# Attention heads on Trainium2: seven bf16 products in 64-row halves of the array instead of nine (or eight) in column strips

## The chip, the cores and the metric

The kernel runs on one core of one Trainium2 chip. The metric is the device time of one execution in microseconds (us); three runs of the kernel before took 1992.37 to 1998.57 us, median 1994.11.

## The reference, cut to what matters

A chain of four layers on 2048 tokens of width 128. Layers 0 and 3 have multi-head attention with 16 heads of width 8 over all 2048 tokens (layer 0 without a mask, layer 3 causal with rotary positions); layers 1 and 2 have attention over wide heads and mixtures of experts. The change touches only the multi-head attentions:

```python
N_HEAD = 16
q = proj(Wq, bq)                 # (heads, 2048, 8)
k = proj(Wk, bk)
v = proj(Wv, bv)
scores = jnp.einsum('bhtd,bhsd->bhts', q, k) * scale
attn = jax.nn.softmax(scores, axis=-1)
out = jnp.einsum('bhts,bhsd->bhtd', attn, v)
```

## The kernel before

`attention_heads(layer, causal)` does one of these attentions. TensorE (PE) multiplies bf16 numbers, so every fp32 query and key is held as a sum of three bf16 parts, and a score is a sum over products of parts stacked in the contraction dimension: 3 x 3 parts x 8 = 72 rows (`STK`), and 3 more rows (75) that subtract the row maximum. For each head three things are made:

- **Maxima** (`fill`, tile `pM`): scores with queries as output rows, reduced over keys by VectorE (DVE) in `take`. Layer 0 uses only the first 64 of the 72 rows: one run is two blocks of 512 keys, block 0 from rows 0 to 63 of `ks`/`qs`, block 1 from rows 64 to 127 of the copies `kd`/`qd`, so that the two matmuls run in two halves of the array. There are 32 runs for each head and four banks (`FILLED`), that is room for two runs. Layer 3 has 40 runs of one block of 128 to 512 columns and three banks.
- **Scores** (`score_chunk`, tile `pS`, a ring of three banks): keys as output rows, 512 queries in a chunk. ScalarE (ACT) takes the exponential of each chunk into `probs`. A chunk may be scored when the exponential three chunks earlier is done. `by_columns` writes a chunk as four matmuls of 32 output columns each, all of them over rows 0 to 74. In layer 3 the maxima go through `by_columns` too, and a block on the diagonal gets a further product `ident_b` x `neg_below`.
- **Sums** (`sum_unit`, tile `pO`): the exponentials times the values in fp32, four chunks at once, each in its own strip of 32 columns over all 128 rows. It waits for the exponential of the fourth chunk of its unit.

A unit is four chunks and one sum: 16 units a head in layer 0, 10 in layer 3. The order of PE is written out in `one_head` of the tensor block: sum of unit u, then the four chunks that lie three ahead, with maxima of the next head (`ahead(u)`) at the places `behind`: in layer 0 both runs after the second score when u is even, after the first and after the third when u is odd. So the three chunks in the ring at the time of a sum are those of the next unit, and the fourth of that unit is the first score after the sum.

When the maxima of a head are complete they are split in three bf16 parts, turned by PE (`turn`), copied by ACT (`keep_rows`), and copied by SyncE (SP) into rows 72 to 74 of the query stack (`load_max_rows`, three DMAs, awaited as `rows_in` before the next head's first score). Nine chunks lie between the turn and that score. SP also loads the stacks of the head after next (`load_stacks`, 14 DMAs a head in layer 0, 8 in layer 3). For the first head of a layer `load_first_keys` issues key loads from SP and ACT; only the last of them waits for the memset of the rows of ones.

```python
TURN_AT = first_chunk[TURN_UNIT + 1] + RING     # 55 of 64 chunks in layer 0, 31 of 40 in layer 3
```

## Time and profile before

| what | value |
|---|---|
| median of 3 runs | 1994.11 us |
| span of the profiled execution | 1923.2 us |
| median less span: what lies around the span | 70.9 us |
| PE, DVE, ACT busy | 1697.7, 1435.9, 1143.8 us |
| one head of layer 0, steady | 40.21 us |
| one head of layer 3, mean of 14 | 26.23 us |

The busy time of PE is modelled: each matmul is shown with its way through the array, some 0.17 us beyond the time in which its columns enter. Distances between the starts of matmuls say more than their lengths. Changes are reckoned on the span and taken over to the median unchanged.

### The profile page before, as it was taken

The page shows a single profiled execution, that of the slowest core. Times are in us where ns is not written, and L with a number is a line of the kernel's source. Part 1 is how long each engine was busy: PE and PEld are TensorE (multiplying, and loading weights), DVE is VectorE, ACT ScalarE, POOL GpSimd, SP SyncE. Part 2 cuts the span into 40 slices and gives each one's busy share as a digit, 9 for nine tenths or more (in the row PEclk, how much of TensorE's full clock was granted, in tenths as well). Part 3 has the DMA queues.
Part 4 walks back from the last instruction along what each step waited for, and adds up shares of the span by engine and source line. Part 5 has one row for each costly group of instructions (what it writes and reads, how often), then busy time and mean ns, then how long its engine had stood idle before and what let it go on. Part 6 is the DMA issues. An engine that isn't in the chain of part 4 may idle for free. (4 is left out here: it accounts for less than half of the span.)

```text
span 1923.2 us, 44062 instructions
## 1 busy us (share of the span) xinstructions
PE 1697.7 (88%) x17529; PEld 802.7 (42%) x17529; DVE 1435.9 (75%) x2718; ACT 1143.8 (59%) x2262; POOL 307.7 (16%) x460
## 2 busy tenths in 40 slices
PE   3799999999999995889997798892779999999977
PEld 2222222222222222434444544781425555555556
DVE  5889999999999954665555507656779999999735
ACT  3268888888888894332222244452317777777754
POOL 0103000010000100000000345443012232210123
PEclk8789999999999998799997899996759999999988
DMA  4112111121111012033233269861511111111132
GB/s 143 36 30 81 63 55 51 55 81 64 55 51 34 28 28 59 33 66 106 95 89 144 69 225 333 268 186 48 191 33 30 33 37 37 34 36 36 28 76 70
DMA packets 78037, 154.52 MB, mean 80 GB/s; under 512 B 18684, under 2 KB 35964, under 8 KB 74136
## 3 DMA queue, kind: packets, MB, share of 16 engines
q1 hardware_dynamic: 63034, 121.38, 20.0%
q0 software_dynamic: 14384, 29.29, 4.9%
q8 instruction: 139, 2.28, 0.5%
q10 hardware_dynamic: 414, 1.04, 0.2%
q14 instruction: 66, 0.54, 0.1%
HBM read 102.23 MB, written 48.89 MB: 79 GB/s over the span
## 5 line engine op out<-in xcount | busy, mean ns | idle before, releaser
L856 ACT ACTIVATE heads_probs<-heads_pS 128x512 f32<-128x512 f32 (+3 forms) x1664 | 851.6, 573 | 187.9 <-PE heads_pS L725 172.2
L881 DVE TENSOR_REDUCE heads_run_max<-heads_pM 128x1 f32<-128x1024 f32 x512 | 592.6, 1216 | 54.6 <-PE heads_pM L747 53.3
L787 PE MATMUL heads_pO<-heads_probs,heads_vh 128*32 128x512 f32 (+2 forms) x3328 | 438.1, 570 | 3.2 <-ACT heads_probs L856 1.4
L725 PE MATMUL heads_pS<-heads_qs,heads_ks 75*32 75x512 bf16 (+3 forms) x4160 | 392.7, 370 | 3.8 <-ACT heads_probs L856 1.6
L892 DVE TENSOR_REDUCE heads_run_max<-heads_pM 128x1 f32<-128x512 f32 x384 | 246.7, 684 | 17.2 <-PE heads_pM L725 13.7
L725 PE MATMUL heads_pS<-heads_q_first,heads_ks 75*32 75x512 bf16 x2496 | 234.4, 377 | 7.9 <-ACT heads_probs L856 7.4
L725 PEld LDWEIGHTS heads_pS<-heads_qs,heads_ks 75*32 75x32 bf16 x4160 | 117.3, 95 | 171.2 <-issue 81.3
L725 PE MATMUL heads_pM<-heads_ks,heads_qs 72*32 72x512 bf16 (+3 forms) x1600 | 174.6, 359 | 1.1 <-DVE heads_run_max L892 0.5
L889 DVE CUSTOM_DVE_ANT_0 heads_masked_out<-heads_pM,heads_mask_end 128x128 bf16<-128x128 f32 (+3 forms) x256 | 120.7, 485 | 19.5 <-PE heads_pM L725 17.2
L787 PEld LDWEIGHTS heads_pO<-heads_probs,heads_vh 128*32 128x32 f32 x3328 | 106.7, 110 | 53.3 <-issue 7.1
L725 PEld LDWEIGHTS heads_pS<-heads_q_first,heads_ks 75*32 75x32 bf16 x2496 | 71.3, 95 | 122.4 <-ACT heads_probs L856 66.8
L1404 ACT ACTIVATE top_act_gate<-top_pG 128x512 f32<-128x512 f32 x68 | 40.6, 597 | 137.3 <-PE top_pU L1360 137.3
L617 POOL DMA_DIRECT2D k_head_out_dram<-heads_ot x120 | 62.9, 531 | 356.9 <-DVE heads_ot L912 230.4
L747 PE MATMUL heads_pM<-heads_ks,heads_qs 64*128 64x512 bf16 x320 | 114.3, 393 | 4.7 <-DVE heads_run_max L881 4.7
L747 PE MATMUL heads_pM<-heads_kd,heads_qd 64*128 64x512 bf16 x320 | 114.3, 393 | 0.0
L725 PE MATMUL heads_pM<-heads_ks,heads_q_first 72*32 72x512 bf16 (+3 forms) x960 | 106.7, 383 | 7.9 <-DMA heads_ks<-k_parts_dram 6.7
L1438 DVE TENSOR_TENSOR top_hidden<-top_act_gate,top_pU 128x512 f32<-128x512 f32 x68 | 46.7, 687 | 76.8 <-ACT top_act_gate L1404 76.8
L2115 POOL DMA_INDIRECT k_x_slots_dram<-k_xn,k_place_i x32 | 31.1, 973 | 381.6 <-DVE k_place_i L1984 358.3
L725 PE MATMUL heads_pS<-k_neg_below,k_ident_b 128*32 128x128 bf16 x1024 | 90.7, 222 | 0.0
L1616 DVE TENSOR_REDUCE second_row_max<-second_banks 128x1 f32<-128x2048 f32 (+15 forms) x16 | 20.7, 1291 | 90.4 <-PE second_banks L1574 90.4
L725 PEld LDWEIGHTS heads_pM<-heads_ks,heads_qs 72*32 72x32 bf16 x1600 | 62.5, 97 | 59.3 <-DVE heads_run_max L892 19.1
L747 PEld LDWEIGHTS heads_pM<-heads_ks,heads_qs 64*128 64x128 bf16 x320 | 29.6, 93 | 133.4 <-DVE heads_run_max L881 86.7
(388 smaller groups left out, 2369.0 us busy)
## 6 DMA issues: line engine op xcount, KB each, us to landing
top_weights<-k_comb_dram SPq DMA_DIRECT2D x128, 128.0 KB, 3.0
second_w<-in_L_W_dram SPq DMA_DIRECT2D x12, 1024.0 KB, 10.8
k_hid_slots_dram<-k_zeros SPq DMA_DIRECT2D x8, 1152.0 KB, 5.0
k_h_slots_dram<-second_work SPq DMA_DIRECT2D x48, 192.0 KB, 3.1
second_work<-k_hid_slots_dram SPq DMA_DIRECT2D x48, 192.0 KB, 4.3
k_parts_dram<-proj_part SPq DMA_DIRECT2D x12, 512.0 KB, 4.1
heads_ks<-k_parts_dram SPq DMA_DIRECT2D x63, 96.0 KB
heads_qs<-k_parts_dram SPq DMA_DIRECT2D x40, 96.0 KB
```

Source lines behind the costliest of these rows:

```text
L617: queue.dma_start(K.head_out[h, :, b * BLK:(b + 1) * BLK], ot[c][b * 32:b * 32 + HD + 1, 0, :])\
L725: mm = pe.matmul(out[cols, :], still[:, cols], moving, start=start, stop=stop)
L747: mm = pe.matmul(pM[:, bank_of(c, j, k), 0:w], (qs, qd)[k][c % ROUND][rows, i * P:(i + 1) * P], (ks, kd)[k][c % ROUND][rows, b * BLK:b * B ...
L787: mm = pe.matmul(pO[k * 32:k * 32 + VW, int(second), o:BLK], vh[c][:, t, :], probs[u % 2][:, k * BLK + o:(k + 1) * BLK], start=first_chunk ...
L856: act.activation(probs[u % 2][:, k * BLK + c0 - b * BLK:(k + 1) * BLK], pS[:, slot, 0:c1 - c0], ACT.Exp)\
L881: dve.reduce_max(run_max[:, i, blocks[0][0] // 2:blocks[0][0] // 2 + 1], both.rearrange("p k c -> p (k c)"), AX.X).then_inc(taken, 2)
L889: dve.tensor_tensor_reduce(masked_out[:, i % TPB, 0:w], pM[:, bank, 0:w], mask_end[:, BLK - w:BLK], 1.0, LOWEST, ALU.add, ALU.max, run_max ...
L892: dve.reduce_max(run_max[:, i, b:b + 1], pM[:, bank, 0:w], AX.X).then_inc(taken, 1)
L1404: act.activation(act_gate[:, m % 2, :], pG[:, m % 2, :], ACT.Silu).then_inc(gated, 1)
L1438: mix = dve.tensor_tensor(hidden[:, m % 2, :], act_gate[:, m % 2, :], pU[:, m % 2, :], ALU.mult)
L1616: chain(dve.reduce_max(self.row_max[:, i:i + 1], self.scores_row[:, 0:(i + 1) * P], AX.X))
L2115: pool.indirect_dma_start(out=K.x_slots[k], out_offset=bass.IndirectOffsetOnAxis(ap=K.place_i[:, c, t:t + 1], axis=0), in_=K.xn[:, t, :], ...
```

## The change

Seven products of parts take the place of nine: query parts 0, 1, 2 with key part 0, the same with key part 1, and query part 0 with key part 2, so 56 rows and 3 for the maximum. Each stack stands twice, in rows 0 to 63 and in rows 64 to 127 of the same tile, and `kd`/`qd` are gone. Every score and every maximum is one matmul of 59 or 56 rows and 128 columns, and successive ones go alternately to the two halves. The masked diagonal takes two products of 64 rows in the half of its score. In layer 0 both runs of maxima of a unit now always stand after the second score. Ten loads a head fill the stacks (half of the queries' rows in one DMA with a repeat), six DMAs bring the rows of the maximum, the rows of ones are set by two memsets, and every first key load waits for one of them.

```diff
-STK = PARTS * PARTS * HD
+PRODUCTS = (3, 3, 1)
+STK = sum(PRODUCTS) * HD
+HALF = 64
...
+            for to, at in ((slice(0, HALF), slice(HALF, P)), (slice(HALF, P), slice(0, HALF))):
+                dve.tensor_copy(K.ident_swapped[to, :], K.ident[at, :]).then_inc(made, 1)
+                dve.tensor_scalar(K.neg_below_swapped[to, :], masks[at, 1, :], NEG, None, ALU.mult).then_inc(made, 1)
...
+def query_loads(K, h):
+
+    yield 0, 2 * PARTS * HD, K.parts[0][h].rearrange("a d t -> (a d) t").unsqueeze(0).broadcast_to([2, PARTS * HD, T])
+    yield 2 * PARTS * HD, STK, K.parts[0][h, 0]
+
+
+def key_loads(K, h):
+
+    for part, n in enumerate(PRODUCTS):
+        at = sum(PRODUCTS[:part]) * HD
+        yield at, at + n * HD, K.parts[1][h, part].unsqueeze(0).broadcast_to([n, HD, T])
...
-        LOADS = 8 if causal else 14
+        LOADS = 10
...
+            half = (0, HALF)[turn]
+            queue.wait_ge(ones_set[0], turn + 1)
+            for row, end, src in key_loads(K, 0):
+                queue.dma_start(ks[0][half + row:half + end, :], src).then_inc(stacked[0], 16)
...
             def load_max_rows(c):
-                for a in range(PARTS):
-                    sp.dma_start(qs[c % ROUND][STK + a:STK + a + 1, :].rearrange("o (t c) -> o t c", c=P),
-                                 max_rows[a * NT:(a + 1) * NT, :]).then_inc(rows_in, 16)
+                for row in (STK, HALF + STK):
+                    for a in range(PARTS):
+                        sp.dma_start(qs[c % ROUND][row + a:row + a + 1, :].rearrange("o (t c) -> o t c", c=P),
+                                     max_rows[a * NT:(a + 1) * NT, :]).then_inc(rows_in, 16)
...
+            turns = itertools.cycle((0, HALF))
...
+                for k, (b, w) in enumerate(blocks):
+                    at = next(turns)
+                    rows = slice(at, at + STK)
+                    mm = pe.matmul(pM[:, bank_of(c, j, k), 0:w], qs[c % ROUND][rows, i * P:(i + 1) * P],
+                                   ks[c % ROUND][rows, b * BLK:b * BLK + w], start=True, stop=True)
...
-                mm = by_columns(pS[:, slot, 0:c1 - c0], ks[c % ROUND][0:STK + PARTS, u * P:(u + 1) * P],
-                                qs[c % ROUND][0:STK + PARTS, c0:c1], True, not diag)
+                at = next(turns)
+                rows, mask = slice(at, at + STK + PARTS), slice(at, at + HALF)
+                mm = pe.matmul(pS[:, slot, 0:c1 - c0], ks[c % ROUND][rows, u * P:(u + 1) * P],
+                               qs[c % ROUND][rows, c0:c1], start=True, stop=not diag)
                 if diag:
-                    mm = by_columns(pS[:, slot, 0:P], K.ident_b[:, :], K.neg_below[:, :], False, True)
+                    pe.matmul(pS[:, slot, 0:P], K.ident_b[mask, :], K.neg_below[mask, :], start=False, stop=False)
+                    mm = pe.matmul(pS[:, slot, 0:P], K.ident_swapped[mask, :], K.neg_below_swapped[mask, :], start=False,
+                                   stop=True)
...
-                        behind = [(len(new) // 2, 1 + 2 * i)[u % 2] for i in range(len(todo))]
+                        behind = [len(new) // 2] * len(todo)
...
-            dve.memset(ks[0][64:96, :], 1.0).then_inc(ones_set[0], 1)
+            for row in (HALF // 2, HALF + HALF // 2):
+                dve.memset(ks[0][row:row + HALF // 2, :], 1.0).then_inc(ones_set[0], 1)
```

PE in the middle of a layer-0 head, before: an even and an odd unit, from sum to sum (`32x512` is a strip of 32 output columns, `128x512` the whole width).

```order
L787 MATMUL heads_pO<-heads_probs,heads_vh 32x512 x4
L725 MATMUL heads_pS<-heads_qs,heads_ks 32x512 x4
L747 MATMUL heads_pM<-heads_ks,heads_qs 128x512
L747 MATMUL heads_pM<-heads_kd,heads_qd 128x512
L725 MATMUL heads_pS<-heads_qs,heads_ks 32x512 x8
L747 MATMUL heads_pM<-heads_ks,heads_qs 128x512
L747 MATMUL heads_pM<-heads_kd,heads_qd 128x512
L725 MATMUL heads_pS<-heads_qs,heads_ks 32x512 x4
L787 MATMUL heads_pO<-heads_probs,heads_vh 32x512 x4
```

The same place after the change: every unit reads so.

```order
L786 MATMUL heads_pO<-heads_probs,heads_vh 32x512 x4
L768 MATMUL heads_pS<-heads_qs,heads_ks 128x512 x2
L742 MATMUL heads_pM<-heads_ks,heads_qs 128x512 x4
L768 MATMUL heads_pS<-heads_qs,heads_ks 128x512 x2
L786 MATMUL heads_pO<-heads_probs,heads_vh 32x512 x4
```

The strips of the sum now stand alone between matmuls of half the rows; before, scores and sums were both in strips of 32 columns, and the maxima stood alone.

PE in layer 3, the last chunk of one unit with its mask, the sum, and the first chunks of the next, before.

```order
L725 MATMUL heads_pS<-heads_qs,heads_ks 32x384 x4
L725 MATMUL heads_pS<-k_neg_below,k_ident_b 32x128 x4
L725 MATMUL heads_pM<-heads_ks,heads_q_first 32x512 x4
L787 MATMUL heads_pO<-heads_probs,heads_vh 32x128 x2
L787 MATMUL heads_pO<-heads_probs,heads_vh 32x512 x2
L725 MATMUL heads_pS<-heads_qs,heads_ks 32x512 x4
L725 MATMUL heads_pM<-heads_ks,heads_q_first 32x256 x4
```

The same place after.

```order
L768 MATMUL heads_pS<-heads_qs,heads_ks 128x384
L771 MATMUL heads_pS<-k_neg_below,k_ident_b 128x128
L772 MATMUL heads_pS<-k_neg_below_swapped,k_ident_swapped 128x128
L742 MATMUL heads_pM<-heads_ks,heads_q_first 128x512
L786 MATMUL heads_pO<-heads_probs,heads_vh 32x128 x2
L786 MATMUL heads_pO<-heads_probs,heads_vh 32x512 x2
L768 MATMUL heads_pS<-heads_qs,heads_ks 128x512
L742 MATMUL heads_pM<-heads_ks,heads_q_first 128x256
```

Here everything was in strips before; now each sum again stands alone between matmuls of half the rows, and the order of the work is the old one.

## Rows read from the trace of the kernel before

**Rows 1.** Windows: a head of layer 0, the start of the last one, a head of layer 3.

```profile
core 0: us, PE busy (x) PEld busy (x) DVE busy (x) ACT busy (x) POOL busy (x), PEclk, DMA share, GB/s
340.90:381.11 40.21, 40.21 (x453) 11.53 (x452) 37.29 (x34) 35.37 (x67) 3.21 (x9) 1.00 0.18 61
700.00:716.00 16.00, 13.62 (x173) 4.15 (x169) 1.05 (x2) 14.98 (x31) 2.91 (x8) 1.00 0.06 14
1611.33:1637.39 26.06, 25.86 (x469) 14.41 (x468) 23.96 (x64) 19.02 (x42) 7.39 (x11) 1.00 0.13 35
```

**Rows 2.** Timeline, PE, two units of layer 0: start, length, what, count.

```profile
322.15 1.03 PE L787 MATMUL heads_pO<-heads_probs,heads_vh 128*32 128x512 f32 x8
323.01 0.39 PE L725 MATMUL heads_pS<-heads_qs,heads_ks 75*32 75x512 bf16 x4
323.33 0.39 PE L747 MATMUL heads_pM<-heads_ks,heads_q_first 64*128 64x512 bf16 x1
323.65 0.62 PE L725 MATMUL heads_pS<-heads_qs,heads_ks 75*32 75x512 bf16 x8
...
326.14 0.39 PE L747 MATMUL heads_pM<-heads_ks,heads_q_first 64*128 64x512 bf16 x1
...
326.37 0.38 PE L747 MATMUL heads_pM<-heads_ks,heads_q_first 64*128 64x512 bf16 x1
...
327.12 1.03 PE L787 MATMUL heads_pO<-heads_probs,heads_vh 128*32 128x512 f32 x8
```

**Rows 3.** Timeline, ACT and DVE, the same two units.

```profile
323.45 2.23 ACT L856 ACTIVATE heads_probs<-heads_pS 128x512 f32<-128x512 f32 x4 [0.21 <-PE heads_pS L725]
...
321.67 4.62 DVE L881 TENSOR_REDUCE heads_run_max<-heads_pM 128x1 f32<-128x1024 f32 x4 [0.36 <-PE heads_pM L747]
```

**Rows 4.** Timeline, last head of layer 0, where no maxima are left.

```profile
702.96 6.42 ACT L856 ACTIVATE heads_probs<-heads_pS 128x512 f32<-128x512 f32 x12
...
703.61 0.40 PE L725 MATMUL heads_pS<-heads_qs,heads_ks 75*32 75x512 bf16 x4 [0.27 <-ACT heads_probs L856]
...
703.83 1.03 PE L787 MATMUL heads_pO<-heads_probs,heads_vh 128*32 128x512 f32 x8
...
704.69 0.82 PE L725 MATMUL heads_pS<-heads_qs,heads_ks 75*32 75x512 bf16 x12
...
706.01 1.03 PE L787 MATMUL heads_pO<-heads_probs,heads_vh 128*32 128x512 f32 x8
```

**Rows 5.** Timeline, ACT's copies of the turned maxima: one a head.

```profile
139.85 0.27 ACT L837 ACTIVATE heads_max_rows<-heads_pS 48x128 bf16<-48x128 bf16 x1 [0.30 <-PE heads_pS L757]
...
662.57 0.27 ACT L837 ACTIVATE heads_max_rows<-heads_pS 48x128 bf16<-48x128 bf16 x1 [0.30 <-PE heads_pS L757]
...
1453.60 0.27 ACT L837 ACTIVATE heads_max_rows<-heads_pS 48x128 bf16<-48x128 bf16 x1 [0.71 <-PE heads_pS L757]
...
1820.81 0.27 ACT L837 ACTIVATE heads_max_rows<-heads_pS 48x128 bf16<-48x128 bf16 x1 [0.82 <-PE heads_pS L757]
```

**Rows 6.** Timeline, SP and PE, from the turned maxima to the next head's scores.

```profile
1611.62 1.82 SPq L639 DMA_DIRECT2D heads_qs<-heads_max_rows  x3
...
1611.07 0.22 PE L757 MATMUL heads_pS<-k_ident_b,heads_max_parts 128*128 128x128 bf16 x1
...
1616.06 0.60 PE L725 MATMUL heads_pS<-heads_qs,heads_ks 75*32 75x512 bf16 x4
```

**Rows 7.** The tile of the maximum's rows, whole run: time to landing.

```profile
DMA to landing us min/median/max: 1.6/1.7/4.7
```

**Rows 8.** Timeline, starts of layer 0's and of layer 3's heads.

```profile
47.34 2.07 ACTq L600 DMA_DIRECT2D heads_kd<-k_parts_dram  x3
...
47.83 1.76 DVE L917 MEMSET heads_ks<- 32x2048 bf16 x1 [3.47 <-PEq L65]
49.46 0.60 ACT L974 ACTIVATE heads_probs<-heads_pS 128x512 f32<-128x512 f32 x1 [11.00 <-PE heads_pS L958]
...
1401.71 1.85 PE L725 MATMUL heads_pM<-heads_ks,heads_q_first 72*32 72x128 bf16 x24 [6.71 <-DMA heads_ks<-k_parts_dram]
```

More of the change, by code:

```diff
@@ L7 @@
+import itertools
 from contextlib import ExitStack
@@ L462, in _ @@
                     dve.tensor_tensor(dst, src, bv.unsqueeze(1).broadcast_to([P, TPB, D]), ALU.add).then_inc(vkept, 1)
-HALF = 64
-PRODUCTS = ((0, 0, 3), (1, 0, 3), (2, 0, 2), (2, 2, 3))
-def first_queries(K, causal):
-    at = 0
-    for _, n0, n1 in PRODUCTS:
-        rows = at + (n1 - n0) * HD
-        for first in (0,) if causal or at >= HALF else (0, HALF):
-            yield K.first_q[first // HALF][first + at:first + rows, :], K.parts[0][0, n0:n1].rearrange("a d t -> d a t")
-        at = rows
+def query_loads(K, h):
[5 more added lines that the diff above has]
+        yield at, at + n * HD, K.parts[1][h, part].unsqueeze(0).broadcast_to([n, HD, T])
+def first_queries(K, causal):
+    for half in (0, HALF):
+        for row, end, src in query_loads(K, 0):
+            yield K.first_q[half + row:half + end, :], src
 def causal_plan(causal):
@@ L581, in load_stacks @@
         def load_stacks(p, c):
[L583 to L600 removed]
+            h = ROUND * p + c
+            for half in (0, HALF):
+                for row, end, src in query_loads(K, h):
+                    yield qs[c % ROUND][half + row:half + end, :], src, stacked[c % ROUND]
+                for row, end, src in key_loads(K, h):
+                    yield ks[c % ROUND][half + row:half + end, :], src, stacked[c % ROUND]
+        def load_first_keys(queue, turn):
+            half = (0, HALF)[turn]
+            queue.wait_ge(ones_set[0], turn + 1)
+            for row, end, src in key_loads(K, 0):
+                queue.dma_start(ks[0][half + row:half + end, :], src).then_inc(stacked[0], 16)
         def split_max(queue, g):
@@ L661, in _ @@
             load_max_rows(0)
-            sp.wait_ge(ones_set[2], 1)
+            sp.wait_ge(ones_set[2], 2)
             every_head(one_head)
@@ L705, in _ @@
             for i in range(1, ROUND):
-                pool.memset(ks[i][64:96, :], 1.0).then_inc(ones_set[i], 1)
-                pool.wait_ge(ones_set[i], 1)
+                for n, row in enumerate((HALF // 2, HALF + HALF // 2)):
+                    pool.memset(ks[i][row:row + HALF // 2, :], 1.0).then_inc(ones_set[i], 1)
+                    pool.wait_ge(ones_set[i], n + 1)
             for i in range(ROUND):
@@ L720, in _ @@
         def _(pe):
-            def by_columns(out, still, moving, start, stop):
-                for g in range(P // VW):
-                    cols = slice(g * VW, (g + 1) * VW)
-                    mm = pe.matmul(out[cols, :], still[:, cols], moving, start=start, stop=stop)
-                return mm
+            turns = itertools.cycle((0, HALF))
             def bank_of(c, j, k):
```

45 lines of the change are left out of this document (9 added, 36 removed).

## The prediction

> **What bounds the kernel now.** I read the windows of one head in each of the two layers first, then the timeline of PE within it, then ACT and DVE beside it. In layer 0 a head takes 40.21 us and PE is shown busy for all of it, DVE for 37.29, ACT for 35.37 [rows 1]. Since the busy time of PE is modelled, I count distances between starts. A chunk of scores takes 0.22 (703.61 to the sum at 703.83), a sum 0.86 (703.83 to 704.69) [rows 4], a pair of maxima 0.23 (326.14 to 326.37) [rows 2]. From scores to maxima it is 0.32 (323.01 to 323.33) and from maxima to scores again 0.32 (323.33 to 323.65) [rows 2], so PE loses some 0.10 wherever strips of 32 columns and halves of rows meet, and nothing between scores and sums, which are both strips. Two units then hold 8 x 0.22 + 2 x 0.86 + 4 x 0.22 + 6 x 0.10 = 4.96 us; from sum to sum over two units the trace shows 327.12 - 322.15 = 4.97 [rows 2]. PE is the limit and waits for nobody. DVE takes four runs in 4.62 and stands idle 0.36 [rows 3], 2.31 a unit; PE's unit is 2.485.
>
> In layer 3 a head takes 26.06 with DVE busy for 23.96 and ACT for 19.02 [rows 1]; the mean of 14 heads is (1820.81 - 1453.60) / 14 = 26.23 [rows 5]. All of PE's work there is in strips, without any change of form, and DVE has only 2.1 us of air. Layer 0's steady heads are 13 intervals of (662.57 - 139.85) / 13 = 40.21 [rows 5].
>
> **Layer 0, work of PE.** Two successive scores, or a pair of maxima, now run in two halves, and the maxima show the price: 0.22 for two [rows 2]. A unit is 0.86 for the sum, 4 x 0.22 for eight halves and two changes of form around the sum, 1.94 us in place of 2.485. That is below DVE's 2.31 and below ACT, whose twelve exponentials take 6.42, so 0.54 apiece and 2.16 a unit [rows 4]. Whether the change gives 2.31 is decided by a chain, not by a sum of work.
>
> **Layer 0, the chain through the sum.** Call T the end of the last exponential of a unit. The score that takes its bank and the sum behind it both wait for T. The last head, which has no maxima, shows this chain in strips: exponential from 702.96, 0.60 long as the exponential in [rows 8] is, to 703.56; score 703.61; sum 703.83; next score 704.69 [rows 4]; ACT starts 0.44 after a score (323.01 to 323.45) [rows 2, 3] and ends 0.60 later. So 0.05 + 0.22 + 0.86 + 0.44 + 0.60 = 2.17, and from sum to sum it is 706.01 - 703.83 = 2.18 [rows 4]. After the change the sum is a strip form between two half forms, so 0.10 is lost ahead of it and 0.10 behind it, both on this chain: 2.38 us. This exceeds DVE's 2.31, and I take it as the new unit. The maxima fit: both runs stand behind the second score after the sum, some 1.5 us after T, and DVE needs the first of them about 2.0 after T; the second can wait for its banks until 2.1, since the last score of the unit waits for the next T anyway. A head is 16 x 2.38 plus the 0.45 that the turn costs now (40.21 - 16 x 2.485), 38.5: 1.7 less, for 15 heads -25.6. The last head has no maxima to gain by and goes from 2.18 to 2.38 a unit: +3.2. Layer 0: -22.4.
>
> The price of the change of form around an fp32 sum is not in the trace; the nearest rows are strips to halves and back in bf16, 0.10 each [rows 2]. Its bounds are 0, if weights and columns of the next form can enter while the sum runs out, and the whole way through the array, 0.39 - 0.22 = 0.17 [rows 2]. I take 0.10. The Trainium skill (TensorEngine Tiling (Array Packing), Key Properties) says that changing the tiling mode drains TensorE. By that rule each sum pays twice; the trace agrees for the maxima, with 0.10 a change. The same skill's page TensorE: Matmul & The Clock Gate (LDWEIGHTS) makes a weight load as long as its columns, an estimate of 107 ns for 128 and 27 ns for 32 columns; no sum here needs it.
>
> **Layer 3.** Per unit up to four maxima stand behind the scores, one of them just ahead of the sum. The chain was 0.05 + 0.44 (score and maximum) + 0.86 + 0.44 + 0.60 = 2.39; after, score and maximum run together (0.22) and two changes come in (0.20): 2.37, the same. What is gained is work of PE, so that maxima stand ready earlier; DVE's 23.96 a head [rows 1] bounds that, at about 24.3 with the turn. Against it: on a diagonal block the second mask product has to follow the first in the same half, where four strips worked at once, so the blocks with masks (16 a head) no longer pair with the maximum behind them; and DVE's three banks are not refilled during a sum, now 1.06 long. Between 24.3 and 27.0 I take 25.7, -0.5 for 15 heads, -7.5. The last head: ten units at +0.20, +2. Layer 3: -5.5.
>
> **The rows of the maximum.** Three DMAs take SP 1.82 to issue [rows 6], 0.61 each; three more put the last issue at 1611.62 + 5 x 0.61 = 1614.67, and it lands 1.7 later [rows 7], at 1616.4, where the next head's first score stood at 1616.06, 4.99 after the turn at 1611.07 [rows 6]. In layer 0 the chain puts that score about 5.0 after the turn, too. The wait of 0.3 to 0.4 lies ahead of two scores that wait for a later exponential anyway, with some 0.5 of air, so a median landing costs nothing; the longest was 4.7 [rows 7] and there are now twice as many. I put +2 for the whole kernel; the bound is 0.4 for 30 heads, +12. Queued behind them on SP are only loads that are needed a head later.
>
> **The starts.** First key loads wait for memsets of 1.76 each [rows 8], the second one done 3.5 after DVE starts; ACT, which issued its loads from 47.34 and did its first exponential at 49.46 [rows 8], now starts issuing about 51.4 and is free at 53.4, 4 us later. Part of this hides behind PE's slow first products, so I take +2.6 in layer 0, where 0 and 4 are the ends. Four query loads in place of seven let the stage before end some 1 earlier: -1. In layer 3 PE waited for the keys until 1401.71 [rows 8] with nothing beside it: one more memset and one more issue by ACT, +3.4 (1.76 + 0.61 at the least). Four small operations of DVE on the constants: +0.5. Fewer rows are loaded a head in layer 0 and more in layer 3, all a head ahead: nothing. Starts: +5.5.
>
> **The sum.** -22.4 - 5.5 + 2 + 5.5 = -20.4 us on the span of 1923.2, so 1902.8; with the 70.9 around it, the median of 1994.11 becomes 1974 (-1.0%). About 0.3%, 6 us, is what a measurement of this kernel can tell from no change.
>
> **The rivals.**
>
> *DVE's floor is reached* (15 in 100). If halves can enter while the sum runs out, the chain is 2.18 and DVE's 2.31 counts: heads of 37.6 in layer 0 (-2.6 x 15 = -39), no loss in the last ones, and 24.5 in layer 3 (-1.7 x 15 = -26); with +7.5 this gives 1937. For it: two pairs of one form follow each other at 0.23 [rows 2]. Against it: every change of form that the trace shows cost 0.10.
>
> *Layer 3 gives back what layer 0 gains* (17 in 100). If DVE starves during the sums and masks block the maxima, a head takes 27.0: +0.8 x 15 + 2 = +14, and 1994.11 - 22.4 + 14 + 7.5 = 1993, no change. For it: DVE has 2.1 us of air in a head of ten units [rows 1], and a sum with its two changes, during which nothing reaches it, grows by 0.20 a unit, 2.0 in all. Against it: before, a maximum waited behind each score, and now it runs beside it.
>
> *Slower: the change of form around the sums is dearer* (22 in 100). There are 16 x 16 + 16 x 10 = 416 sums with two changes each, 832 in all, nearly all on the chain. At 0.15 instead of 0.10 that is +42: 2015. It decides from 0.125 on, where the gain of 20.4 is gone. For it: fp32 needs two passes of weights for a sum, each shown as four loads, which the bf16 changes don't have. Against it: the weight loads of both kinds are short beside the columns.
>
> *The clock of PE falls.* It was 1.00 of 2.4 GHz with PE entering columns for (0.86 + 0.88) / 2.18 = 80% of the time in the last head [rows 1, 4]; after, it is 1.74 / 2.38 = 73%. I give this 1 in 100: at 1.2 GHz a unit of layer 0 would be about 3.6 us.
>
> **How the numbers follow.** The forecast has 45 in 100, DVE's floor 15, no gain 17, slower 23 with the clock in it. The forecast's own range is 1962 to 1986, by 0.09 to 0.115 a change of form. The whole range, leaving 8 in 100 of the floor and 11 of the slower case outside, is 1948 to 2008. Faster by over 0.3%: 0.45 + 0.15 + some 0.02 of the third case = 0.62; within 0.3%: the other 0.15; slower: 0.23.
>
> **What would show it.** In a middle head of layer 0: sums 2.38 apart, 0.32 from a score's start to the sum and 0.96 from the sum to the next score, intervals of 38.5 between copies of the turned maxima, DVE busy 37.3, PE's start distance of successive scores near 0.01 where both banks are free. In layer 3: intervals near 25.7, more waits of DVE for maxima during sums. At the heads' starts 2.6 and 3.4 later first maxima, counted from the stage's start. The prediction is wrong if sums in layer 0 are 2.31 or over 2.45 apart, or if layer 3's heads grow.

## The result, and the profile after

The changed kernel takes 2004.12 us (median of 5 runs, 1996.05 to 2005.03), the kernel before 1994.11 on the same chip: ratio 1.0051 [1.0032, 1.0071]. It is slower by 10 us where the prediction said 1974.0, 20 faster. On another chip, where the kernel before takes 1924.12, it takes 1950.55: 1.0139 [1.0116, 1.0161]. The chips of all experiments below take 1924 to 1926 us for the kernel before, and the span of 1923.2 in the rows ahead of the prediction fits such a chip and not the one of the result. The "70.9 us around the span" were therefore no part of the program but the distance between two chips: the profiled execution of the changed kernel has a span of 1994.2 in 1996.05, and the kernel before has one of 1922.1 in 1923.95 (e4), so 1.9 lie around it. Times below are set against the kernel before on the same chip.

Windows of a head of layer 0 and of one of layer 3, changed kernel (columns as in [rows 1]):

```profile
350.00:389.30 39.30, 35.94 (x261) 7.78 (x257) 37.51 (x34) 33.90 (x67) 3.21 (x9) 1.00 0.16 57
1706.68:1732.63 25.95, 23.31 (x195) 7.66 (x194) 23.92 (x64) 18.51 (x41) 3.45 (x7) 1.00 0.13 42
```

PE's work is smaller (35.94 in 39.30, where it filled 40.21 [rows 1]), and the head is 0.9 shorter, not 1.7. Timeline of PE, one unit in the middle of a head of layer 0, against [rows 2]:

```profile
320.71 1.07 PE L786 MATMUL heads_pO<-heads_probs,heads_vh 128*32 128x512 f32 x8
321.71 0.39 PE L768 MATMUL heads_pS<-heads_qs,heads_ks 59*128 59x512 bf16 x2
321.93 0.91 PE L742 MATMUL heads_pM<-heads_ks,heads_q_first 56*128 56x512 bf16 x4
322.67 0.49 PE L768 MATMUL heads_pS<-heads_qs,heads_ks 59*128 59x512 bf16 x2
323.10 1.07 PE L786 MATMUL heads_pO<-heads_probs,heads_vh 128*32 128x512 f32 x8
```

From sum to sum it is 2.39, from a sum to the next score 1.00 in place of 0.86. ACT and DVE beside it, against [rows 3]: ACT waits 0.33 once a unit, and DVE runs on without a gap that the view shows.

```profile
322.13 2.06 ACT L855 ACTIVATE heads_probs<-heads_pS 128x512 f32<-128x512 f32 x4 [0.33 <-PE heads_pS L768]
```

```profile
320.04 11.92 DVE L880 TENSOR_REDUCE heads_run_max<-heads_pM 128x1 f32<-128x1024 f32 x10
```

The last head of layer 0, against [rows 4]: 2.39 from sum to sum where it was 2.18, with nothing but scores and sums on PE. A score is followed by the sum 0.32 later (717.08 to 717.40) and the sum by a score 0.99 later.

```profile
714.69 0.39 PE L768 MATMUL heads_pS<-heads_q_first,heads_ks 59*128 59x512 bf16 x1 [0.47 <-ACT heads_probs L855]
715.01 1.06 PE L786 MATMUL heads_pO<-heads_probs,heads_vh 128*32 128x512 f32 x8
...
717.08 0.39 PE L768 MATMUL heads_pS<-heads_q_first,heads_ks 59*128 59x512 bf16 x1 [0.47 <-ACT heads_probs L855]
717.40 1.06 PE L786 MATMUL heads_pO<-heads_probs,heads_vh 128*32 128x512 f32 x8
718.39 0.60 PE L768 MATMUL heads_pS<-heads_q_first,heads_ks 59*128 59x512 bf16 x3
```

The rows of the maximum, SP and PE, against [rows 6]: six issues take 4.17, and the first score of the next head that needs them waits 0.92.

```profile
190.66 4.17 SPq L643 DMA_DIRECT2D heads_qs<-heads_max_rows  x6
...
196.38 0.39 PE L768 MATMUL heads_pS<-heads_qs,heads_ks 59*128 59x512 bf16 x1 [0.92 <-DMA heads_qs<-heads_max_rows]
```

The start of layer 0's heads, against [rows 8]: two memsets instead of one and from 52.30 on (47.83 before), ACT's loads at 56.34 and its first exponential at 58.35 (49.46 before), and PE's first maxima at 66.63, after a wait of 4.79 for the keys.

```profile
52.30 1.76 DVE L917 MEMSET heads_ks<- 32x2048 bf16 x1 [6.88 <-PEq L68]
54.55 1.76 DVE L917 MEMSET heads_ks<- 32x2048 bf16 x1 [0.48 <-issue]
...
56.34 1.97 ACTq L603 DMA_DIRECT2D heads_ks<-k_parts_dram  x3
58.35 1.57 ACT L974 ACTIVATE heads_probs<-heads_pS 128x512 f32<-128x512 f32 x3 [18.84 <-issue]
...
66.63 1.04 PE L742 MATMUL heads_pM<-heads_ks,heads_q_first 56*128 56x512 bf16 x4 [4.79 <-DMA heads_ks<-k_parts_dram]
```

ACT's copies of the turned maxima, one a head, are milestones; the first of layer 0 and the last of layer 3 (against [rows 5]):

```profile
107.75 0.27 ACT L836 ACTIVATE heads_max_rows<-heads_pS 48x128 bf16<-48x128 bf16 x1 [19.26 <-PE heads_pS L752]
...
1888.44 0.27 ACT L836 ACTIVATE heads_max_rows<-heads_pS 48x128 bf16<-48x128 bf16 x1 [0.73 <-PE heads_pS L752]
```

Read in this way, the span of each kernel falls into five stretches. This table, in us, is worked out from those rows and the spans, one execution of each kernel, all on chips where the kernel before takes 1924 to 1926:

| kernel | to first | 15 heads, layer 0 | last of 0 to first of 3 | 15 heads, layer 3 | rest | span |
|---|---|---|---|---|---|---|
| before (e4) | 94.8 | 607.0 | 722.3 | 396.9 | 101.1 | 1922.1 |
| changed (e5) | 107.5 | 594.8 | 738.3 | 405.3 | 102.4 | 1948.3 |
| old form of loads (e1) | 99.0 | 595.9 | 730.6 | 399.4 | 102.3 | 1927.3 |
| starts relieved (e6) | 95.3 | 593.4 | 727.7 | 402.1 | 103.3 | 1921.8 |
| rows by half (e7) | 95.6 | 585.6 | 727.9 | 396.1 | 103.5 | 1908.7 |
| e7, old layer 3 (e8) | 95.8 | 586.0 | 725.9 | 398.7 | 101.0 | 1907.3 |
| full strips at the sums, apart (e15) | 96.2 | 575.6 | 723.8 | 398.0 | 103.1 | 1896.8 |

Three kernels whose layer 3 runs unchanged code (e4, e8, and the profile ahead of the prediction) differ by up to 2.5 us in its heads (396.2 to 398.7), so a difference of that size between two rows says nothing. The heads of layer 0 do get shorter (-12.2), the way to the first of them 12.7 longer, that to layer 3's first 16.0, and layer 3's heads 8.4 longer. The theory with which I went into the experiments: the mechanism in layer 0 is the predicted one, and what eats it is how the stacks and the rows of the maximum are brought. The rival: the matmuls in halves are themselves dearer than thought.

### The profile page after: what moved, and what is told of

Same layout as the page of the kernel before. It is cut to its first block and busy times, and to the rows that moved or that the text cites. A ratio compares the mean times of both kernels' runs of the same rounds, so it can differ in the third digit from the quotient of the medians.

```text
span 1994.2 us, 29288 instructions
## 1 busy us (share of the span) xinstructions
PE 1618.9 (81%) x10105; PEld 647.7 (32%) x10105; DVE 1446.2 (73%) x2724; ACT 1117.0 (56%) x2262; POOL 314.4 (16%) x464
## 5 line engine op out<-in xcount | busy, mean ns | idle before, releaser
L768 PE MATMUL heads_pS<-heads_qs,heads_ks 59*128 59x512 bf16 (+3 forms) x1040 | 263.5, 373 | 28.8 <-ACT heads_probs L855 13.3
L742 PE MATMUL heads_pM<-heads_ks,heads_qs 56*128 56x512 bf16 (+3 forms) x1040 | 248.2, 380 | 40.4 <-DVE heads_run_max L880 13.6
L742 PE MATMUL heads_pM<-heads_ks,heads_q_first 56*128 56x512 bf16 x624 | 157.1, 399 | 57.4 <-DMA heads_ks<-k_parts_dram 27.1
L768 PE MATMUL heads_pS<-heads_q_first,heads_ks 59*128 59x512 bf16 x624 | 160.7, 379 | 21.2 <-ACT heads_probs L855 17.4
L768 PEld LDWEIGHTS heads_pS<-heads_qs,heads_ks 59*128 59x128 bf16 x1040 | 75.9, 93 | 289.8 <-ACT heads_probs L855 264.4
L742 PEld LDWEIGHTS heads_pM<-heads_ks,heads_qs 56*128 56x128 bf16 x1040 | 64.1, 94 | 138.7 <-DVE heads_run_max L880 105.0
L768 PEld LDWEIGHTS heads_pS<-heads_q_first,heads_ks 59*128 59x128 bf16 x624 | 45.1, 94 | 185.7 <-ACT heads_probs L855 173.3
L786 PEld LDWEIGHTS heads_pO<-heads_probs,heads_vh 128*32 128x32 f32 x3328 | 66.1, 108 | 98.2 <-issue 79.1
L1359 PE MATMUL top_pG<-k_xnT,k_gate 128*128 128x512 f32 x128 | 67.0, 606 | 4.2 <-PEq L68 4.2
L1368 PE MATMUL top_pY<-top_hidden,k_down 128*128 128x512 f32 x128 | 65.8, 595 | 1.6 <-DVE top_hidden L1444 1.6
```

What stands on the lines that cost most here:

```text
L742: mm = pe.matmul(pM[:, bank_of(c, j, k), 0:w], qs[c % ROUND][rows, i * P:(i + 1) * P], ks[c % ROUND][rows, b * BLK:b * BLK + w], start=Tru ...
L768: mm = pe.matmul(pS[:, slot, 0:c1 - c0], ks[c % ROUND][rows, u * P:(u + 1) * P], qs[c % ROUND][rows, c0:c1], start=True, stop=not diag)
L786: mm = pe.matmul(pO[k * 32:k * 32 + VW, int(second), o:BLK], vh[c][:, t, :], probs[u % 2][:, k * BLK + o:(k + 1) * BLK], start=first_chunk ...
L1359: pe.matmul(pG[:, m % 2, :], gw, x, start=True, stop=True)
L1368: pe.matmul(pY[:, b % 2, :], w, hidden[:, m % 2, :], start=(n == 0), stop=(n == L1_J)).then_inc(downed, 1)
```

## The experiments

All are compared with the kernel before on their own chip.

**e1, the loads alone put back.** The stacks keep the new halves, but their rows are ordered as before, so that each load has 8 as its outermost dimension (12 loads a head).

```diff
-    yield 0, 2 * PARTS * HD, K.parts[0][h].rearrange("a d t -> (a d) t").unsqueeze(0).broadcast_to([2, PARTS * HD, T])
-    yield 2 * PARTS * HD, STK, K.parts[0][h, 0]
+    for part, n in enumerate(PRODUCTS):
+        at = sum(PRODUCTS[:part]) * HD
+        yield at, at + n * HD, K.parts[0][h, 0:n].rearrange("a d t -> d a t")
...
-        yield at, at + n * HD, K.parts[1][h, part].unsqueeze(0).broadcast_to([n, HD, T])
+        yield at, at + n * HD, K.parts[1][h, part].unsqueeze(1).broadcast_to([HD, n, T])
```

> The changed kernel with its stack loads in the form of the kernel before: each load takes its rows with the eight head dimensions outermost (12 DMAs a head in place of 10), so that it isn't two or three long rows of packets. Theory 'loads': in the changed kernel's trace the first keys of layer 0 were awaited until 66.6 us (55.3 before) while 26 packets of 159 ns landed in each 2 us, about two of 16 DMA engines at work; the stores of the key parts ended the stage before 4.5 us later; in layer 3 the rows of the maximum were awaited up to 3.3 us. All this is the form of the loads: this run should be 15 to 30 us below the changed kernel, that is 1975 to 1990, with layer 0's first turned maxima near 100 us instead of 107.75. Rival 'memsets and more DMAs for the rows of the maximum': the loads' form is innocent, the waits stay, 2000 to 2006.

Measured 1933.3 us, ratio 1.0041 [1.0024, 1.0058], where the changed kernel has 1.0139: the form of the loads costs 18.5 us (medians less those of their own kernel before) or 21 (spans). At layer 0's start PE gets its first maxima at 58.85 after a wait of 0.74 for the keys; in e5 it was 67.03, after 3.27. Windows of 54 to 60 us show why (columns as in [rows 1]; the seventh is the share of the 16 DMA engines), first the changed kernel, e5:

```profile
54.00:60.00 6.00, 3.09 (x5) 1.03 (x4) 1.56 (x3) 1.57 (x3) 5.71 (x10) 0.78 0.22 67
```

and then e1:

```profile
54.00:60.00 6.00, 3.99 (x12) 1.50 (x12) 0.64 (x1) 3.37 (x6) 2.90 (x8) 1.00 0.45 158
```

67 GB/s against 158 with loads of the same stacks under way: 0.22 of 16 is 3.5 engines busy for the queues of SP and ACT together, 0.45 is 7.2. The window does not meet the same point of both starts, since SP issues its first key load at 53.18 in e5 and at 50.18 in e1; but later it is no better in e5:

```profile
60.00:64.00 4.00, 3.75 (x5) 1.01 (x3) 0.00 (x0) 1.40 (x3) 0.08 (x1) 0.50 0.24 83
```

Of the 8.2 us by which PE gets its maxima later, 3.0 lie ahead of the stage: its first memset starts at 51.39 in e5 and at 48.39 in e1. In the stage before, the first query loads and the stores of the key parts are under way together, and the slowest store lands 9.6 us after its issue in e5 (tile `k_parts_dram`, 28 to 52 us),

```profile
DMA to landing us min/median/max: 3.8/4.4/9.6
```

and 6.9 in e1:

```profile
DMA to landing us min/median/max: 3.8/4.3/6.9
```

**e2, the places of the maxima alone**, in the kernel before: `behind = [len(new) // 2] * len(todo)`.

> The kernel before with one part of the change alone: in layer 0 both runs of maxima always stand behind the second score. By the count of form changes (0.10 us each, two fewer per unit of odd number: 4 instead of 6 for two units) a unit falls from 2.485 to 2.385 us, a head of layer 0 from 40.2 to 38.6, in all -1.6 x 15 = -24 us: 1970. If form changes weren't what the time goes to, or DVE starves with both runs in one place, no change or slower: 1994 or more.

Measured 1936.0, ratio 1.005 [1.0031, 1.0068]: slower, and my expectation fell. Timeline of PE, e2:

```profile
362.69 0.39 PE L747 MATMUL heads_pM<-heads_ks,heads_qs 64*128 64x512 bf16 x1
362.69 0.39 PE L747 MATMUL heads_pM<-heads_kd,heads_qd 64*128 64x512 bf16 x1
363.18 0.39 PE L747 MATMUL heads_pM<-heads_ks,heads_qs 64*128 64x512 bf16 x1
```

The second run follows 0.49 after the first, not 0.23. Its weight load shows what it waits for, a bank that DVE is still reducing:

```profile
363.17 0.09 PEld L747 LDWEIGHTS heads_pM<-heads_ks,heads_qs 64*128 64x128 bf16 x1 [0.39 <-DVE heads_run_max L881]
```

PE, which was the limit, waits with it, in every second unit (in the others the second run follows after 0.26). Heads take 40.87.

**e3, the places alone put back**, in the changed kernel.

> The changed kernel with the maxima of layer 0 at the old places (after the second score, or after the first and the third). In 64-row halves a maximum costs no change of form, so the place should not matter to TensorE, and by the chain through the sum (2.38 us a unit) the time stays that of the changed kernel within 3 us (2001 to 2007). If the placement carries the gain of layer 0 by giving VectorE its banks together, this one is over 5 us slower.

Measured 1951.96, ratio 1.0132 [1.0114, 1.015], where the changed kernel has 1.0139: the places are worth nothing there, since a unit in the old places takes 2.39 too. That is what a chain through the sum asks for, and not a limit by DVE or by PE's work.

**e4 and e5, both kernels again.**

> The kernel before, unchanged, for its profile beside the others. The profile shown of it has a span of 1923.2 us where its timed runs took 1992 to 1999, and the changed kernel's profile has 1994.2 for a time of 1996.05. If the shown profile was an execution of another kind, this one shows where the 70 us lie (between the layers' heads: 783 us from the last turned maxima of layer 0 to the first of layer 3 in the changed kernel, 722 in the profile shown of before); if it is again near 1923, the 70 us lie around the span.

Measured 1923.95, with a span of 1922.1. The span is again near 1923, but the time is as well, so the 70 us lie between the chips and not around the span.

> The changed kernel once more, unaltered, beside the kernel before and the three below on one chip, as their base. Its parts so far: layer 0's heads -9 to -11 us, last head of layer 0 and start of layer 3 +17, start of layer 0 +8 to +12. Expected 9 to 14 us over the kernel before of the same chip, with the first turned maxima of layer 0 some 12 us later than before and of layer 3 some 17 us later counted from the last of layer 0. If it stands within 3 us of the kernel with the old form of loads (+8), the form of the loads costs nothing and that theory falls.

Measured 1950.55, 26 us over the kernel before, beyond what I expected. Against e1 the first turned maxima are 8.5 later, the way to layer 3 is 7.7 and its heads are 5.9 longer.

**e6, the starts relieved** (on e1): half of the ones is set by POOL beside DVE, key part 0 waits for no ones, and in layer 0 SP issues all first keys.

> The loads in the old form (six of the queries and six of the keys a head, outermost dimension 8), and the starts relieved: the ones of the second half are set by POOL beside DVE, only the loads of key parts 1 and 2 wait for ones, and in layer 0 all first keys are issued by SP, so that ACT is free. Theory that the two memsets and ACT's late issues are on the path: layer 0's first turned maxima 3 to 4 us earlier than with the loads alone (which stood 4.3 behind the kernel before), layer 3's 2 to 3 earlier; in all 4 to 6 less than the loads alone, about +2 to +4 against the kernel before. Rival, that the path at the starts goes through the stage before and the arrival of the keys: no more than 1 us.

Measured 1925.68, ratio 1.0009 [0.9999, 1.0019]: 6.3 us less than e1 by the medians less those of their own kernel before, 5.5 by the spans, 3.8 of it at layer 0's start. The start of layer 0 now stands 0.5 behind the kernel before.

**e7, rows by half** (on e6): two semaphores, one for each copy of the maximum's rows; a score waits for that of its own half, and the half that is needed first is issued first.

```diff
-                if n == 0:
-                    pe.wait_ge(rows_in, 32 * PARTS * (h + 1))
+                if n <= 1:
+                    half = HALF_OF[h, n]
+                    pe.wait_ge(rows_in[half // HALF], 16 * PARTS * (h + 1))
```

> As the kernel with relieved starts, and a score waits only for the three rows of the maximum of its own half; the half of the head's first score is brought first. Theory that six loads of rows in a row (some 4.1 us on SP) make PE wait once a head: the waits for rows go from about 1.0 to 0.2 us a head in layer 0, the interval of heads from 39.4 to about 38.8 to 39.0; in all 6 to 10 us less than the kernel with relieved starts, so 3 to 7 under the kernel before. Rival, that ACT's four copies of the sums and the turn set the end of a head: the interval stays at 39.3 or above and the time within 2 us.

Measured 1911.69, ratio 0.9938 [0.9916, 0.9959]: 14 us less than e6 and faster than the kernel before. Waits of PE's weight loads for the rows between 110 and 720 us (us in total, times, longest), e6:

```profile
PEld heads_pS L773 <- DMA heads_qs<-heads_max_rows: 10.0, 10, 1.7
```

and e7:

```profile
PEld heads_pS L809 <- DMA heads_qs<-heads_max_rows: 2.7, 5, 0.9
```

Every third head has its queries in `heads_q_first`, where the waits go from 3.4 in 5 to 1.3 in 3.

The heads of layer 0 settle at 38.64, a hair over the 38.5 of the prediction; layer 3's 15 heads take 6.0 less.

**e8, layer 3 as before the change** (on e7: nine products in strips there, three rows of the maximum).

> Layer 0 as in the kernel with rows by half; layer 3 wholly as before the change (72 and 75 rows in strips, single stacks, three rows of the maximum, 8 loads, no swapped constants). Theory that layer 3 gains nothing from the change and loses at its start and in its early heads: layer 3's first turned maxima again as far from layer 0's last as before plus 2 to 3 for layer 0's last head (722 to 725 us), intervals 26.0 as before; in all 8 to 13 us less than the kernel with rows by half, and 10 to 18 under the kernel before. If it is less than 4 under the kernel with rows by half, layer 3 in the new form costs nothing and the loss lies elsewhere.

Measured 1909.45, ratio 0.9925 [0.9905, 0.9944]; only 2.2 less than e7, and my expectation of 8 to 13 fell. Once loads and rows are mended, layer 3's heads take 396.1 in the new form (e7) and 398.7 in the old one, where the old one took 396.9 in e4, so no gain can be told from the scatter; around them the new form takes some 4.5 more.

**e9, strips around the sums** (layer 0, on e7): the score ahead of a sum and the one behind it are four strips of 32 columns over 59 rows.

```diff
+                if strips:
+                    mm = by_columns(pS[:, slot, 0:c1 - c0], ks[c % ROUND][rows, u * P:(u + 1) * P],
+                                    qs[c % ROUND][rows, c0:c1], True, not diag)
...
-                            score_chunk(p, d, n)
+                            score_chunk(p, d, n, strips=not causal and k in (0, len(new) - 1))
```

> On the kernel with rows by half: in layer 0 the score just ahead of each sum and the one just behind it are written as four strips of 32 columns over their 59 rows, the other two scores of the unit and the maxima stay whole in halves. So the two changes of form of a unit no longer touch the sum. Theory that the two changes around the sum lie on the chain at 0.10 each: the last head's unit falls from 2.39 to 2.18, in the other heads the chain falls to 2.18 too and DVE (about 2.31 a unit) or PE decides, so heads of 37.3 to 37.7 in place of 38.64; in all 16 to 22 us less than the kernel with rows by half. Rival, that something else (bank waits for DVE, ACT) holds the unit at 2.39: the last head falls, the others do not, 3 us less.

Measured 1972.54, ratio 1.0239 [1.0219, 1.0259]: 59 us more than e7 by medians, 62 by spans, the opposite of what both theories said. Timeline of PE, e9:

```profile
323.33 0.38 PE L823 MATMUL heads_pS<-heads_qs,heads_ks 59*128 59x512 bf16 x1
323.64 0.40 PE L771 MATMUL heads_pS<-heads_qs,heads_ks 59*32 59x512 bf16 x4
323.96 1.07 PE L841 MATMUL heads_pO<-heads_probs,heads_vh 128*32 128x512 f32 x8
324.96 0.40 PE L771 MATMUL heads_pS<-heads_qs,heads_ks 59*32 59x512 bf16 x4
325.29 0.39 PE L823 MATMUL heads_pS<-heads_qs,heads_ks 59*128 59x512 bf16 x1
```

From a strip over 59 rows to the sum it is 0.32, and 1.00 back: as dear as from a half of full width. And the edge to the halves costs its 0.10 as well (324.96 to 325.29), so a unit has four changes. Units take 2.53 and 2.78 by turns. The longer ones hold a wait that is no change of form: their second run of maxima waits for a bank of DVE's, as in e2, 0.24 longer than in the others.

```profile
320.56 0.10 PEld L788 LDWEIGHTS heads_pM<-heads_ks,heads_q_first 56*128 56x128 bf16 x2 [0.48 <-DVE heads_run_max L935]
...
323.10 0.10 PEld L788 LDWEIGHTS heads_pM<-heads_ks,heads_q_first 56*128 56x128 bf16 x2 [0.24 <-DVE heads_run_max L935]
```

So of the 0.27 that a unit lost against 2.39, about 0.12 belong to the places of the maxima, and the 59 us are not the price of the changes alone.

**e10, strips in both layers**, and in layer 3 the last maximum ahead of the last score.

> As the kernel with strips around the sums of layer 0, and the same in layer 3, where also the maximum that stood between the last score of a unit and the sum now stands ahead of that score. Theory that layer 3 gained nothing because the maximum ahead of the sum waits for a bank of DVE's and holds the sum back: heads of 24.8 to 25.5 in place of 25.95, 8 to 15 us less than with strips in layer 0 alone. Rival, that DVE with its 23.8 us and its empty times decides layer 3: heads stay at 25.8 to 26.0 and the time within 3 us.

Measured 2032.36, ratio 1.0558 [1.0534, 1.0582]: layer 3's heads take 30.03, 4.1 more for ten units with two more changes each. At 0.10 a change that would be 2.0, and the moved maximum has a share of 0.2 (e11); where the rest lies was not looked into.

**e11, the last maximum of a unit ahead of the last score**, layer 3, on e7.

> On the kernel with rows by half, without strips: in layer 3 alone the maximum that stood between the last score of a unit and the sum stands ahead of that score. If the bank wait ahead of the sum is what layer 3 lost its gain to: heads of 25.2 to 25.6 in place of 25.95, 5 to 11 us less than the kernel with rows by half. If only the number of maxima that DVE can take decides: within 2 us. Slower by up to 5 us if the last score now waits behind the bank.

Measured 1917.86, ratio 0.9958 [0.9944, 0.9972], 5 us more than e7, heads 26.18 instead of 25.95: my expectation of 5 to 11 less fell. The case with "slower by up to 5 us" holds, in which the last score waits behind the bank.

**e12, the new form of loads alone**, in the kernel before.

> The kernel before with nothing changed but the order of rows in its stacks: part first, so that its loads have an outermost dimension of 2 or 3 with rows of 4 KB, as the changed kernel's. Theory that this form alone costs the starts (it took 17 us there): first turned maxima of layer 0 some 8 us later than before, layer 3's start another 8, in all 14 to 20 us over the kernel before. Rival, that it costs only together with the waits for two memsets: under 5 us.

Measured 1932.26, ratio 1.0032 [1.0022, 1.0041], +7 us, between theory and rival. Layer 0's start is 5.0 later (99.8 against 94.8), layer 3's 2.5. In the changed kernel the same form took 18 to 21; there every first key load also stands behind a memset, layer 3's heads have six key loads in place of four, and the query load [2, 24, 2048], whose outermost dimension is 2, is not in e12 at all. The late start of the stage may belong to that load: in e12 the first memset of layer 0 starts at 47.01, no later than before (47.34). The rest was not tried apart.

**e13, strips over both halves.** The two scores at a sum are strips over rows 0 to 122, so over both copies at once (the five rows between are set to zero), and their exponential halves its argument. Otherwise as e9.

```diff
+                    both = slice(0, HALF + STK + PARTS)
+                    mm = by_columns(pS[:, slot, 0:c1 - c0], ks[c % ROUND][both, u * P:(u + 1) * P],
+                                    qs[c % ROUND][both, c0:c1], True, True)
...
+                                   scale=0.5 if twice(n) else 1.0).then_inc(exped, 1)
```

> On the kernel with rows by half: in layer 0 the two scores next to each sum are strips of 32 columns again, this time over rows 0 to 122, that is over both copies of the stack at once (five rows between them are zeros), and their exponential halves its argument. Theory that a form is rows and columns together: strips over 123 rows and the sum over 128 are one form, so from such a score to the sum it is 0.22 and from the sum to the next 0.86; the last head's unit is 2.18, the others 2.27 to 2.40 with DVE as the limit; heads of 36.8 to 38.7, in all 3 to 25 us less than the kernel with rows by half. Rival, that returning to strips costs 0.10 at every edge whatever the rows: as the strips over 59 rows, heads of 42.6, 60 us more.

Timeline of PE, e13, the same place:

```profile
323.87 0.40 PE L780 MATMUL heads_pS<-heads_qs,heads_ks 123*32 123x512 bf16 x4
324.09 1.03 PE L851 MATMUL heads_pO<-heads_probs,heads_vh 128*32 128x512 f32 x8
324.96 0.39 PE L780 MATMUL heads_pS<-heads_qs,heads_ks 123*32 123x512 bf16 x4
325.28 0.39 PE L833 MATMUL heads_pS<-heads_qs,heads_ks 59*128 59x512 bf16 x1
```

0.22 to the sum and 0.87 behind it: strips over 123 rows and over 128 are one form, strips over 59 another. But the time is 1941.1, ratio 1.0081 [1.0052, 1.011]; heads take 40.81, since now the second run of maxima waits for DVE's banks, as in e2, and the strip that has to come before the sum stands behind it: units take 2.42 and 2.64 by turns, again apart by such a wait.

**e14, e13 with the old layer 3.**

> The same layer 0, and layer 3 wholly as before the change. Layer 3 as before was worth 2 us with rows by half; expected 0 to 4 us less than the kernel with full strips in layer 0 and both its copies in layer 3.

Measured 1936.93, ratio 1.0056 [1.0035, 1.0078], 4 less than e13.

**e15 and e16, e13 with other places**: the runs of maxima behind the first and the third score (e15), behind the first and the second (e16).

> As the kernel with full strips in layer 0, the two runs of maxima of a unit apart again: behind the first and behind the third score. If the second run's wait for DVE's banks ahead of the third score is what holds the unit, 5 to 12 us less; but there are two more changes of form a unit only if a strip stands beside a maximum, and the one behind the first score is such an edge already, so no more of those. If a longer stretch without a new maximum during the sum starves DVE, 0 to 10 us more.

Measured 1896.11, ratio 0.9844 [0.9819, 0.987]: 45 us less than e13 (41 by the spans) for a change of places alone. The shortest and most frequent interval of heads is 37.68 (the mean of 13 is 38.14), and the last head is back at 2.18 a unit (699.61, 701.79, 703.97). Window of 40 us in layer 0, e15:

```profile
320.00:360.00 40.00, 39.37 (x379) 10.27 (x375) 39.58 (x36) 36.43 (x71) 3.19 (x9) 1.00 0.16 57
```

DVE is busy for 39.58 of 40: it is the limit at last. The expectation had 5 to 12 us less; the places were worth far more.

> As the kernel with full strips in layer 0, the first run of maxima behind the first score and the second behind the second. DVE gets its first run 0.1 to 0.2 earlier after the sum. If DVE's own time decides (two runs in about 2.27 us), within 2 us of the other places; if its starving during the sum decides, 3 to 8 us less than with both behind the second score.

Measured 1916.02, ratio 0.9949 [0.9934, 0.9965], heads 39.18. The nearer the two runs stand, the longer the head: 37.68, 39.18, 40.81.

**e17, e15 with the old layer 3.**

> Layer 0 with full strips beside the sums and maxima apart, layer 3 wholly as before the change. If layer 3 in the new form costs its 2 to 4 us in starts and early heads, this takes 1892 to 1894 where the kernel before takes 1924 to 1926, a ratio of 0.982 to 0.984; if it costs nothing, 1896.

Measured 1893.48, ratio 0.9826 [0.981, 0.9843], the fastest of all. Three pairs now have the old layer 3 ahead, by 2.2, 4.2 and 2.9 us; the intervals of each pair overlap, so I take it as likely, not as shown.

## Why the prediction was wrong

It was wrong in sign. The step that failed is "Fewer rows are loaded a head ... nothing": the new form of the loads was put at nothing and cost 18 to 21 us. With it alone put back the kernel is still 8 us slower than before (e1), so three further terms had to be off as well, the rows of the maximum above all. The parts, in the order of the sum:

- **Layer 0, the chain through the sum (-22.4): right.** Sums are 2.39 apart where 2.38 was said, 0.32 from score to sum, 1.00 where 0.96 was said from sum to score. So a change ahead of an fp32 sum costs 0.10, as one in bf16 does, and one behind it 0.13 to 0.14; on the chain the two make 0.21 a unit (2.18 to 2.39), where 0.20 was said. e3 shows that the places do not matter while the chain decides; e15 shows that without the two changes the last head returns to 2.18 and, with the maxima apart, the others reach DVE's limit. With the rows mended, 15 heads are 21.4 shorter (e7), where -25.6 was said.
- **Rows of the maximum (+2): the size failed.** "A median landing costs nothing" and "some 0.5 of air" do not hold: e7 took back 13 to 14 us, 7.8 in layer 0's heads and 6.0 in layer 3's. In layer 0 of e5 PE's weight loads waited for the rows 15 times, up to 1.8. Six issues take 3.67 to 4.75 there, 0.61 to 0.79 each, where 0.61 each had been reckoned. Even my bound of +12 was too low. e7 changes two things at once, what a score waits for and which half is brought first; their shares are not known apart.
- **"Fewer rows are loaded a head ... nothing", and the starts (+5.5): the step that failed.** The part on the starts counts memsets and issues, and their size was right: e6 took back 5.5 to 6.3. But it takes the loads by number and by rows, and never asks in which form they come. The outermost dimension of all but the shortest went from 8 to 2 or 3, and that cost 18 to 21 us (e5 against e1), as much as the whole predicted gain: 8.5 up to the first turned maxima of layer 0, 7.7 between the layers' heads and 5.9 in layer 3's heads, less 1.1 in layer 0's. At the starts there is no head ahead of them to hide behind. "Four query loads in place of seven let the stage before end some 1 earlier: -1" failed with it: that stage ended 4.1 later (first memset at 51.39 in e5, 47.34 in e4), and 1.1 later with the old form of the loads (48.39 in e1).
- **Layer 3 (-7.5): the gain did not come.** Steady heads take 25.95, before 26.03, where 25.7 was said. Timeline of PE and DVE in e7:

```profile
1706.30 0.69 DVE L932 TENSOR_REDUCE heads_run_max<-heads_pM 128x1 f32<-128x512 f32 x1 [0.84 <-PE heads_pM L781]
...
1707.66 0.23 PE L781 MATMUL heads_pM<-heads_ks,heads_q_first 56*128 56x128 bf16 x1 [0.22 <-DVE heads_run_max L929]
...
1707.81 1.06 PE L827 MATMUL heads_pO<-heads_probs,heads_vh 128*32 128x512 f32 x8
```

  DVE starves for 0.84 behind a sum, then PE waits for DVE's bank ahead of the next one, so both may lose, in turn, what the faster matmuls gave. That fits the rival *Layer 3 gives back what layer 0 gains*, at a smaller price, but it is argued and not shown: with the bank wait moved (e11) the heads grew. In the changed kernel as it stands the mean of 14 heads went from 26.23 to 26.67, which the prediction named as a sign of being wrong; with the rows mended it is 26.13 (e7).
- **The sum.** -20.4, and +18 to 21 for the form of the loads, +11 for the rows, +7 for layer 3, +4 in layer 0's heads make +20 to +23 against the +26 measured on these chips; 3 to 6 us are not accounted for. By the spans it is 3.6, in the stretches around the heads of e7: 0.8 ahead of layer 0's, 2.4 between the layers (5.6 more than before, of which 3.2 were forecast for the last head) and 0.4 behind layer 3's (2.4 more than before, of which 2 were forecast); that is little more than two executions of one kernel differ.

The rival that was to end slower, a dearer change of form, was not what happened: it was slower for a reason that none of the cases held. That 2004 lies within the whole range of 1948 to 2008 is luck: the room above 1994 was left for that rival.

The Trainium skill had the rule. DMA: Bandwidth & Descriptors (Why a DMA increments its semaphore by 16 and not by 1) says that a transfer is spread over the largest number of engines, up to 16, that divides the slowest dimension of both sides. By that rule it is 2 for [2, 24, 2048] and 3 for [3, 8, 2048], where it was 8 before. The trace agrees in direction: a DMA share of 0.22 against 0.45 in the windows above. The number of engines of a single load is not read from a trace here. I had looked up what a transfer costs, not how many engines its shape gives it.

What stays open: on the chip of the result the change costs 10 us, on another 26. The stretches that the change touches most are alike in both traces of the changed kernel (first turned maxima at 107.75 and 107.50, 15 heads of layer 0 593.8 and 594.8), so the difference may lie in what the kernel before does on that chip; but no trace of it there is at hand, and the one of the changed kernel is of its fastest execution, 1996.05 where the others took 2003 to 2005.

## What to carry to other kernels

Ask of each load that a change rewrites how many DMA engines its outermost dimension gives it, above all of loads with no work ahead of them; fewer loads are no gain by themselves. A row that many matmuls wait for is best awaited by the part that needs it. When the form of matmuls changes, look at each edge between forms, rows and columns both, count those on the chain and not all of them, and then find the places of the other work anew: the kernel with full strips stood 17 us above the kernel before in one placing and 29 below it in another (e13, e15).

## What I had not expected of the hardware

- The form of a matmul is its rows as well as its columns: 32 columns over 59 rows next to 32 columns over 128 rows cost 0.10 ahead of the sum and 0.13 behind it, over 123 rows nothing (0.32 and 1.00 against 0.22 and 0.87; e9, e13). The Trainium skill, TensorEngine Tiling (Array Packing), lists 64 x 32 and 128 x 32 as modes of their own (Available Configurations) and says that changing the mode drains the engine (Key Properties); the trace agrees, with the price above. I had read the rule as one on columns.
- The time of the same program differs by 70 us between chips (1994 and 1924). For the changed kernel the two spans are 1994.2 and 1948.3, and 45 of the 46 us between them lie from layer 0's last turned maxima to layer 3's first (783.3 and 738.3), where a granted clock of 0.81 stands in a stretch (1200 to 1250 us) in which the other chip shows 1.00. PE is also less busy in it (30.25 of 50 us against 45.73), so whether the clock is the cause or follows from late work is not shown.
